# One visit of TensorE to the small tiles per step, with all four head pairs

## The reference

```python
# layer 0
Q = (x @ W_q + b_q).reshape(B, N, H, hd)          # K and V likewise; H = 8, hd = 64
scores = einsum('bihd,bjhd->bhij', Q, K) / sqrt(hd)
soul_bias = (x @ w_g[:D])[:, :, None] + (x @ w_g[D:])[:, None, :] + b_g
attn = softmax(scores + (soul_bias + log(adjacency + EPS))[:, None, :, :], axis=-1)
x = einsum('bhij,bjhd->bihd', attn, V).reshape(B, N, D) + x
# layer 1
q = x @ Wq + bq ; k = x @ Wk + bk
scores = where(mask, -1e18, einsum('bod,bid->boi', q, k) / sqrt(512))
attn = where(mask, 0.0, softmax(scores, axis=2))
x = x + einsum('boi,bie->boe', attn, x) @ Wc
out = (x - mu) * rsqrt(var + 1e-05) * gamma + beta
```

## Time and profile before

| | us |
|---|---|
| median of 3 runs | 2256.19 (2255.06 to 2257.74) |
| the profiled execution | 2256.57 |
| its span in the trace | 2254.7 |
| PE busy | 2238.5 (99%) |
| DVE busy | 1794.6 (80%) |
| ACT busy | 1223.6 (54%) |
| POOL busy | 987.0 (44%) |

### The profile page before, as it was taken

One profiled execution on the slowest core, in us unless ns is written; L12 is line 12 of the kernel. 1 busy time (PEld: TensorE's weight loads), 2 busy tenths in 40 slices (PEclk: granted clock), 3 DMA queues, 4 the chain that ended last, 5 costly groups with the idle time before them and its releaser, 6 DMA issues.

```text
span 2254.7 us, 39435 instructions
## 1 busy us (share of the span) xinstructions
PE 2238.5 (99%) x13258; PEld 1866.8 (83%) x13258; DVE 1794.6 (80%) x5363; ACT 1223.6 (54%) x3489; POOL 987.0 (44%) x1139
## 2 busy tenths in 40 slices
PE   9999999999999999999999999999999999999998
PEld 6788888888888888888888888888888888888886
DVE  6778788778788787887787887878887878878775
ACT  5555555555455555555554565555555545655553
POOL 0244354553445543545434455435454344554343
PEclk9999999999999999999999999999999999999999
DMA  7333333433344333333333433333343334333321
GB/s 244 113 123 117 118 126 127 131 109 127 112 137 127 123 116 123 122 126 129 106 131 110 139 127 122 117 117 128 120 132 109 131 110 139 127 119 121 117 94 57
DMA packets 189659, 277.46 MB, mean 123 GB/s; under 512 B 24593, under 2 KB 126097, under 8 KB 185233
## 3 DMA queue, kind: packets, MB, share of 16 engines
q1 hardware_dynamic: 189168, 274.42, 37.0%
q10 hardware_dynamic: 288, 0.52, 0.1%
HBM read 166.28 MB, written 108.59 MB: 122 GB/s over the span
## 4 chain that ended last, share of the span: by engine, by line
PE 94%; DMA 2%; DVE 2%; SPq 1%; ACT 0%; issue 0%; POOL 0%; DVEq 0%; POOLq 0%
PE bank L256 27%; PE bank L258 26%; PE bank L257 26%; PE bank L509 5%; PE bank L522 5%; PE bank L551 5%; DMA turn_dram<-turned 1%; DMA probsT<-turn_dram 1%; DVE x1n L1255 0%; DVE turned L1185 0%; DMA ident<-in_ident_in 0%; SPq L318 0%; ACT probs L863 0%; SPq L349 0%; DVE probs L1166 0%
## 5 line engine op out<-in xcount | busy, mean ns | idle before, releaser
L1547 POOL TENSOR_TENSOR probs<-probs,rcp 128x512 f32<-128x512 f32 x256 | 290.5, 1151 | 875.0 <-DVE rcp L1176 874.8
L863 ACT ACTIVATE probs<-probs,nmax 128x128 f32<-128x128 f32 x1024 | 397.5, 390 | 159.7 <-DVE nmax L1166 158.3
L1255 DVE STREAM_TRANSPOSE x1n<-x1T 32x512 f32<-32x512 f32 x496 | 348.6, 703 | 38.3 <-DMA out<-x1n 30.8
L1555 POOL TENSOR_TENSOR x_lo<-xT_land,x_hi 128x512 fp32r<-128x512 f32 x124 | 168.9, 1392 | 328.0 <-ACT x_hi L809 328.0
L847 ACT ACTIVATE k_sb<-bank,cols 128x512 f32<-128x512 f32 x128 | 88.2, 689 | 270.8 <-PE bank L551 168.0
L1166 DVE CUSTOM_DVE_ANT_0 probs<-bank,bias 128x128 f32<-128x128 f32 x1024 | 227.2, 286 | 2.8
L256 PE MATMUL bank<-wc_hi,x_hi 128*128 128x512 f32 x512 | 204.3, 399 | 0.0
L256 PE MATMUL bank<-wv_hi,x_hi 128*128 128x512 f32 x512 | 203.2, 397 | 0.6 <-ACT q_sb L852 0.6
L256 PE MATMUL bank<-x_hi,wq_hi 128*128 128x512 f32 x512 | 201.9, 394 | 0.0
L256 PE MATMUL bank<-x_hi,wk_hi 128*128 128x512 f32 x512 | 199.9, 391 | 0.2
L1192 DVE SCALAR_TENSOR_TENSOR x1T<-bank,cols,xT_land 128x512 f32<-128x512 f32 x124 | 93.0, 750 | 134.2 <-PE bank L522 126.8
(11 more groups left out here) (171 smaller groups left out, 5287.3 us busy)
## 6 DMA issues: line engine op xcount, KB each, us to landing
turn_dram<-turned SPq DMA_DIRECT2D x128, 512.0 KB, 2.6
probsT<-turn_dram SPq DMA_DIRECT2D x512, 128.0 KB, 2.7
xn<-in_x SPq DMA_DIRECT2D x126, 256.0 KB, 3.2
xT_land<-in_xT SPq DMA_DIRECT2D x31, 1024.0 KB, 7.4
out<-x1n SPq DMA_DIRECT2D x124, 256.0 KB, 2.0
adj_sb<-in_adj SPq DMA_DIRECT2D x32, 256.0 KB, 3.2
c_rows<-c_dram SPq DMA_DIRECT2D x32, 256.0 KB, 3.2
at_dram<-scratch SPq DMA_DIRECT2D x30, 256.0 KB, 2.0
```

What stands on the lines that cost most here:

```text
L863: op = nc.scalar.activation(probs[:, k, :], probs[:, k, :], ACT.Exp, bias=nmax[:, k:k + 1], scale=-1.0, accum_out=sums[:, k:k + 1])
L1255: op = nc.vector.transpose(x1n[b * BLK:(b + 1) * BLK, :, :] .rearrange("p g (c a s) -> p a c g s", c=C, a=P // BLK)[:, a, :, :, :], x1T[a ...
L1547: nc.gpsimd.tensor_tensor(probs[:, half, :], probs[:, half, :], rcp[:, half].unsqueeze(2).to_broadcast([P, HALF, P]), ALU.mult)\
L1555: nc.gpsimd.tensor_tensor(x_lo[:, c, :], xT_land[(t + 1) % 2][:, c, :], x_hi[:, c, :].bitcast(f32), ALU.subtract).then_inc(s["pool_x"], 1)
```

## The change

One visit is left in a step. It holds pv(u, 0) to pv(u, 3) of the group before and scores(t, 0) to scores(t, 3) of this one. The projections of k and q are taken ahead: those of group t+1 are the last wides of step t. Behind the visit come v of group t, g, the pair scores and y of u, then k and q of t+1 with the four contexts of u between them, so that layer 1 of u ends within step t. q_sb, k_sb and probsT have four buffers in place of two; x1 is written over x in `xT_land` in place of its own buffer, so the x of group t+1 is loaded in four chunks, each once `pair_scores` has read that chunk of x1; the bias is written over `ln_adj`. The first step is written anew (scores of all pairs, v, the product of layer 1's weights, then k and q of group 1; the first row of gates is spread by one matmul instead of a DMA through DRAM), and so is the last. The loops are written out in Python as before.

```diff
         def s_banks(c):
-            return (bank[4], bank[5]) if c % 2 == 0 else (bank[6], bank[7])
+            return ((bank[4], bank[5]), (bank[6], bank[7]), (bank[0], bank[1]), (bank[2], bank[3]))[c]
...
         def g_bank(c, stage):
-            return bank[((2, 3, 0, 1), (0, 1, 4, 5), (6, 7, 3, 2))[stage][c]]
+            return bank[((6, 7, 5, 4), (4, 5, 0, 1))[stage][c]]
...
         def y_bank(g, stage):
-            return bank[((0, 1, 2, 3), (0, 1, 4, 5), (1, 4, 5, 6))[stage][g]]
+            return bank[((2, 3, 6, 7), (5, 0, 1, 2))[stage][g]]
...
+            def visit(t):
+
+                u = t - 1
+                pe.wait_ge(s["act_k"], nth("act_k", t, 2))
+                pv(u, 0)
+                pe.wait_ge(s["act_q"], nth("act_q", t, 2))
+                pv(u, 1)
...
+                    pv(u, c)
+                for c in range(C):
+                    scores(t, c)
+
+            def layer1_begin(t):
+
+                u = t - 1
+                for g in range(3):
+                    project_v(t, g)
+                pe.wait_ge(s["dve_x1"], nth("dve_x1", u, 3))
+                pe.wait_ge(s["dve_max"], nth("dve_max", t, 2))
+                g_whole(u, 0, STEPS)
+                pe.wait_ge(s["dve_max"], nth("dve_max", t, 3))
+                g_whole(u, 1, STEPS)
+                pe.wait_ge(s["act_v"], nth("act_v", t, 1))
+                g_whole(u, 2, STEPS)
+                pe.wait_ge(s["act_v"], nth("act_v", t, 2))
+                g_whole(u, 3, STEPS)
+                project_v(t, 3)
+                pe.wait_ge(s["dve_max"], nth("dve_max", t, 5))
+                for c in range(C):
+                    pair_scores(u, c)
+                pe.wait_ge(s["dve_max"], nth("dve_max", t, 6))
+                y_whole(u, 0, STEPS)
...
+            def step(t):
+
+                u = t - 1
+                visit(t)
+                layer1_begin(t)
+                y_whole(u, 2, STEPS)
+                y_whole(u, 3, STEPS)
+                project_k(t + 1, 0)
+                project_q(t + 1, 0)
...
+            def layer1_begin(t):
+
+                u = t - 1
+                for c in range(C):
+                    residual0(u, c)
+                maxima(t, 0)
+                for c in range(C):
+                    x1lo(u, c)
+                x1_rows(u, 0)
+                recips(t, 0)
+                turn(t, 0)
+                maxima(t, 1)
+                x1_rows(u, 1)
+                x1_rows(u, 2)
+                recips(t, 1)
+                x1_rows(u, 3)
+                turn(t, 1)
+                maxima(t, 2)
+                row_term(u, 0)
+                row_term(u, 1)
+                recips(t, 2)
+                row_term(u, 2)
+                row_term(u, 3)
+                turn(t, 2)
+                maxima(t, 3)
```

More of the change, by code:

```diff
@@ L20 @@
-from collections import namedtuple
 from contextlib import ExitStack
@@ new lines, in first_step @@
+            def first_step():
+                wake()
+                for c in range(2):
+                    project_k(0, c)
+                    project_q(0, c)
+                pe.wait_ge(s["act_k"], nth("act_k", 0, 1))
+                project_k(0, 2)
+                late_projections(0)
+                for c in range(C):
+                    scores(0, c)
+                pe.wait_ge(s_lo["v"], C)
+                for g in range(GG):
+                    project_v(0, g)
+                m_chunk(0)
+                m_chunk(1)
+                m_row_term()
+                m_columns()
+                m_chunk(2)
+                m_chunk(3)
+                pe.wait_ge(s_lo["m"], 1)
+                project_k(1, 0)
+                pe.wait_ge(s_lo["m"], 2)
+                project_q(1, 0)
+                pe.wait_ge(s_cst1, 1)
+                project_k(1, 1)
+                pe.wait_ge(s_cst1, 2)
+                project_q(1, 1)
+                pe.wait_ge(s["act_k"], nth("act_k", 1, 1))
+                project_k(1, 2)
+                late_projections(1)
@@ L802, in _ @@
-            iterations(pe, body)
+            first_step()
+            for t in range(1, NG - 1):
+                step(t)
+            final_step(NG - 1)
         @block.scalar
@@ L973, in final_step @@
                 exps(t, 1, 0)
                 exps(t, 1, 1)
-                q_out(t, 2)
-                k_out(t, 3)
-                q_out(t, 3)
+                v_out(t, 2)
+                g_out(u, 0)
+                g_out(u, 1)
                 exps(t, 2, 0)
-                g_out(u, 0, BEFORE)
                 exps(t, 2, 1)
-                g_out(u, 1, BEFORE)
+                g_out(u, 2)
+                g_out(u, 3)
+                v_out(t, 3)
+                exps(t, 3, 0)
+                exps(t, 3, 1)
@@ new lines, in layer1_begin, with step @@
+                exp1(u)
+                y_out(u, 0)
+            def step(t):
+                u = t - 1
+                layer1_begin(t)
+                next_x_high(t)
+                y_out(u, 1)
+                log_adj(t + 1)
+                att1T_high(u)
+                k_out(t + 1, 0)
+                q_out(t + 1, 0)
+                y_out(u, 2)
+                y_out(u, 3)
+                k_out(t + 1, 1)
+                q_out(t + 1, 1)
+                norm(u, 0)
+                k_out(t + 1, 2)
+                norm(u, 1)
+                q_out(t + 1, 2)
+                norm(u, 2)
+                k_out(t + 1, 3)
+                norm(u, 3)
+                q_out(t + 1, 3)
@@ L1082, in _, with wc_high @@
-            iterations(act, body)
+            def wc_high(d):
+                nc.scalar.activation(w_hi["c"][:, d, :], wc_land(d), ACT.Copy).then_inc(s_hi["c"], 1)
+            first_step()
+            for t in range(1, NG - 1):
+                step(t)
+            final_step(NG - 1)
         @block.vector
```

1138 lines of the change are left out of this document (484 added, 654 removed).

## The result

The changed kernel takes 2444.6 us in the median of four runs (2441.6 to 2449.8), beside 2256.8 for the kernel before: a ratio of 1.0835, with a 95% interval from 1.0822 to 1.0848. The prediction was 2331.5 with a range from 2285 to 2390. The direction is right; the loss was forecast at 75 us and is 188.

What follows compares the result with a forecast made beforehand. PE bounds the kernel; after the change it also waits for DVE's chain, making the period 68.34 + 3.2 = 71.55. Then 85.3 + 30 x 71.55 + 98.2 = 2330.0, plus 1.9, less 0.4: 2331.5 us, range 2285 to 2390.

Steps and rivals of the forecast that it cites:

- the joint visit saves 0.58: PE's joint visit of PV and scores: 7.64 us instead of 8.22, saving 0.58 us a step.
- PE waits for `maxima` at g0, v3 and y0: Behind the visit, PE waits for DVE's maxima about 1.1, 1.0 and 1.0 us, with y0 3.1 late in all.
- The stretch from g0 to y0: DVE's chain behind the visit: maxima ready for g0 at 16.8 us and for y0 at 36.0.
- The first visit: In the first step: the first visit starts at 85.3 us, bounds 84 and 89.
- The last step: From the last visit to the end: 98.2 us against 97.2, with PE idle for 4 us ahead of pv(31, 3).
- the x1lo: Four x1lo on DVE behind maxima(t, 0): 2.6 us, with POOL done with affine at about 5 to 7.
- the end of the step before: End of a step on DVE: residual1(u, 3) ends some 4 us before the next visit.
- Covered by 0.2 us.: At k0 of the next group: split x ready at 48.8 us, PE asks at 49.0; bounds 0 and 1.5 late.
- 71.55: Forecast period of the loop in us: 68.34 + 3.2, against 68.93 before; bounds 71.0 and 75.
- rival 2: Late x, or affine reaching into x1lo and stores into x1_rows: period 73 to 75, time 2375 to 2435; chance 0.17.
- Rival 3: PE's waits of about 1 us bring the lower clock: period 74, time 2405; chance 0.04.
- DVE's share in the 30 us behind a visit: Sign expected in the stretch behind a visit: DVE's busy share over 90%.

Runs made afterwards that it cites:

- DVE's new order: Against the kernel with residual1 and recips(t, 0) moved earlier: DVE's order behind maxima(t, 1) changed so each turn waits behind other work; 2280.2 us, ratio 1.0102.
- the last two kernels: One with x_hi moved ahead of exp1 on ACT, 2259.7 us; then that kernel with next_gate(t + 1, 3) moved behind y_low on DVE, 2239.1 us.
- the last kernel: Against the kernel with x_hi ahead of exp1 on ACT: att1T_low before next_gate(t + 1, 2), next_gate(t + 1, 3) behind y_low on DVE; 2239.1 us, ratio 0.9928.

## Why the prediction was wrong

**Right.** The direction, and the mechanism: the joint visit saves 0.58 (7.64 measured), then PE waits for `maxima` at g0, v3 and y0. The stretch from g0 to y0 was set at 19.2 to 19.3 and is 19.67. The first visit was expected at 85.3 and starts at 84.08. The last step was 98.2 and is 100.6, with a wait of 2.50 for the moves ahead of pv(31, 3), where 4 were expected.

**Wrong: the size of a term, the x1lo.** The prediction took 2.6 us for the four, between 3.2 "while POOL worked" and 2.4 without, "POOL being done with `affine` at about 5 to 7". POOL is done at 9.7, and they take 4.45 on the mean: 1.9 us a step. The bound of 1.2 for one held on the mean (1.1); single ones take up to 1.8, and the four up to 5.1. The 3.2 was too low as a price beside POOL, and the trace of the kernel before had the right one: the pair in the earlier trace rows ran mostly after POOL's last row (`affine` ended at 1059.89), while the pair before it, beside POOL's work from end to end, took nearly twice as long. The mean over all 124 was 1.2 each.

```profile
1044.78 3.09 DVE L1199 TENSOR_TENSOR x_lo<-x1T,x_hi 128x512 fp32r<-128x512 f32 x2
```

**Wrong: the end of the step before.** This step is the cause of the one above. "residual1(u, 3) ends some 4 us before the next visit" had no row of the joint step behind it. There DVE waits 4.54 for xn at the last gate, 1.54 for c_rows ahead of bias, and bias itself takes 3.26 beside affine, so residual1(u, 3) ends 0.1 us behind the visit's start. These are the figures of the step shown. The first two waits are for transfers that take longer in the new step, in which the load of x, the moves and the attention's store stand close together: xn lands after 5.0 us instead of 3.2, at_dram after 5.3 instead of 2.0. That this bunching makes them slow was not tried by itself (with DVE's new order at_dram falls to 3.0, and to 2.0 in the last two kernels, where xn still takes 4.0 to 4.4); that the order of residual1 and of the gate on DVE sets the end was tried, and is shown. It adds 0.65 of waiting for stores at x1_rows, and 0.1 at maxima(t, 0), which in three steps comes late by PE's wait for q ahead of the scores. With the x1lo that is 2.6 us, and g0 comes at 19.4 instead of 16.8.

**Wrong: "Covered by 0.2 us."** From y0 to the next visit go 36.3 instead of 35.45, 0.9 a step. PE's instructions need 35.55 there, as the last kernel's undisturbed steps show, so 0.1 is a sum that was a little short. The other 0.77 arises wholly in the k0 block, 0 to 1.8 in single steps: it is the wait for x_lo that the prediction held to be covered. The page of waits gives only 8.7 us over the run for it, 0.3 a step.

These terms, 2.6 + 0.4 (g0 to y0) + 0.9, are the 3.9 us by which the period of 75.44 exceeds 71.55. Thirty of them are 117 us; the first and last step add 1. That is the miss in the profiled run; the median lies 113 above the forecast.

**The chances.** All of this is rival 2, "The late half binds as well": affine that reaches into the x1lo, the stores into x1_rows, x late. It had 73 to 75 and a chance of 0.17, on margins of 0.2 and 1 us that rested on one wait each. The measured 75.44 is the prediction's worst case, 75 with every bound at its far end, and 0.4 more. These parts are not apart from each other: a late residual1 moves affine, and with it x1lo, the stores and the next residual. So the far ends of the bounds came together, where the forecast took each term near its middle.

**Rival 3** (the clock) happened and cost little: the lower level stands behind g0 in 23 of the 31 steps (0.56 in the window shown), and the mean over the loop is 0.98, above the 0.95 that was named as its sign. But DVE's chain from g0 to y0 covers them. Where it doesn't, the price is 1.6 us a time.

**A sign that did not come:** DVE's share in the 30 us behind a visit is 84%, not over 90%. DVE is the bound there all the same, since what it waits for (PE's scores, POOL, the stores) lies in its own chain. A share of busy time could not have told this.

## What to carry over

An engine that is 81% busy over a step can still be the bound in the stretch behind a visit; the same instructions of DVE, POOL, ACT and SP, ordered otherwise, took this kernel from 8.3% above the one before to 0.7% below it. In costing such a chain, follow the step round to its own start: what ends just ahead of the stretch is still running beside it, and a margin of less than 1 us there was no cover. Each time that a wait was taken away, the next one stood in another queue (POOL, then ACT behind exp1, then a gate that waited for a DMA), so the engine that sits idle with ready work behind a blocked instruction is the one to look for.

## What the runs showed of the hardware

**DVE and POOL beside each other.** x1lo, with two inputs from SBUF, takes 0.68 alone and up to 1.8 beside POOL. row_term, again with two, takes 0.72 or 1.29, and POOL's two multiplications 2.97 beside it; with all row_terms behind maxima(t, 3) none takes over 0.75. Beside transposes, with one input, neither is slowed: 0.69 to 0.71 for each of the changed kernel's 496 transposes, 2.04 for POOL. The bias, 1.49 in the kernel before and 1.50 with affine cut, took 3.26 in the step shown. The Trainium skill ("SBUF — State Buffer", SBUF: two separate sides) says that a DVE instruction with two SBUF inputs and a GpSimd instruction that reads SBUF exclude each other for their whole length; the traces agree, and so what to put on DVE in POOL's shadow is a transpose.

**The clock does not follow from the wait alone.** The granted clock fell behind a wait of 2.09 and not behind one of 1.89 in the run with fewer transposes. In the changed kernel a wait of 3.49 us at g0 is followed by slow wides in one step (1158.92 above; the wides behind it take 0.63 each instead of 0.39) and not in another:

```profile
630.84 0.47 PE L244 MATMUL bank<-x_hi,wm_hi 128*128 128x512 f32 x1 [3.49 <-DVE nmax L1115]
631.15 0.39 PE L245 MATMUL bank<-x_lo,wm_hi 128*128 128x512 f32 x1
```

What else decides it, these runs don't tell.
